# A hybrid network of eight stages on one core: heads and row sums from one product, sums and shifts made inside other stages, router joined with experts, one scan input in sixteen made by VectorE

## The reference

```python
x = L0_attn_a_x
x = x + l0_attn_a(layernorm(x))   # 16-head attention + state-space scan + gated MLP
x = x + l0_ffn(layernorm(x))      # two layers: window attention, gated MLP
x = x + attn_b(layernorm(x))      # 16-head causal attention
x = x + l0_ffn(layernorm(x))
x = x + l1_attn_a(layernorm(x))   # 16-head causal attention, rotary, biases on q, k, v and output
x = x + l1_ffn(layernorm(x))      # 8 experts, the best two of each token count
x = x + l1_attn_b(layernorm(x))   # random features
x = x + l1_ffn(layernorm(x))
# a head of attention (8 features):  softmax(q k^T / sqrt(8)) v
# the scan:   h = exp(dt*A)*h + dt*b*x ;  y = sum(h*c)   over 256 steps, 128 x 128 states
# a window layer first shifts features 64..127 by one token:
#             t2 = pad(t2)[:, :-1] ; h = concat(t1, t2)
# experts:    tgt2 = sum_e gate_e * (relu(x W1_e + b1_e) W2_e + b2_e) ; layernorm(tgt + tgt2)*gamma + beta
```

## Time and profile before

| | us |
|---|---|
| median of three runs (6312.53 to 6316.73) | 6315.28 |
| the profiled execution, its own time | 6308.24 |
| its span, first to last instruction | 6306.2 |
| three attention stages | 302.1, 306.4, 320.8 |
| scan_stage | 1218.0 |
| one window_attention_stage (of four) | 427.3 |
| one experts_stage (of two) | 465.7 |

### The profile page before, as it was taken

How to read it: one execution, slowest core, us unless ns; L and a number is a source line. 1 busy time by engine, 2 the same in 40 slices (tenths; PEclk the granted TensorE clock), 3 DMA queues, 4 the chain that set the end, 5 groups by cost and what they waited for, 6 DMA issues and landing times. The chain is left out here.

```text
span 6306.2 us, 119595 instructions
## 1 busy us (share of the span) xinstructions
PE 5418.4 (86%) x42357; PEld 2908.8 (46%) x42357; DVE 3589.7 (57%) x4103; ACT 3331.1 (53%) x4993; POOL 2512.4 (40%) x1721
## 2 busy tenths in 40 slices
PE   6876888888887998998898998999897999776998
PEld 2432555555544553564344554554343444343443
DVE  4557999999954554554344554554454343554344
ACT  4555888888854553554444554454343333443343
POOL 1223999999933651652122661662221000000000
PEclk8996999999998999999899999999899999998999
DMA  1002111101011110110000110110000210001121
GB/s 41 1 0 77 31 32 30 33 30 33 29 47 29 40 40 14 41 41 13 1 0 18 45 40 12 42 40 20 28 0 8 54 40 13 0 0 27 32 36 27
DMA packets 136966, 171.03 MB, mean 27 GB/s; under 512 B 32352, under 2 KB 85728, under 8 KB 135520
## 3 DMA queue, kind: packets, MB, share of 16 engines
q1 hardware_dynamic: 136800, 168.85, 10.2%
HBM read 80.11 MB, written 12.85 MB: 15 GB/s over the span
## 5 line engine op out<-in xcount | busy, mean ns | idle before, releaser
L2318 POOL TENSOR_TENSOR arena<-arena,wbig 128x1024 f32<-128x1024 f32 x512 | 1191.8, 2515 | 103.5 <-DMA wbig<-scratch_b 100.3
L2305 DVE TENSOR_TENSOR_SCAN arena<-banks,arena 128x1024 f32<-128x1024 f32 x512 | 1141.5, 2279 | 63.7 <-ACT banks L2249 45.5
L944 ACT ACTIVATE arena<-banks,wbig 128x512 f32<-128x512 f32 x512 | 352.0, 688 | 584.3 <-PE banks L907 572.7
L601 DVE TENSOR_REDUCE arena<-banks 128x4 f32<-128x1024 f32 (+1 forms) x384 | 401.9, 1047 | 432.8 <-PE banks L435 305.1
L957 DVE TENSOR_TENSOR arena<-arena 128x512 f32<-128x512 f32 x512 | 353.3, 692 | 490.2 <-ACT arena L944 434.7
L768 POOL TENSOR_TENSOR X<-X,Z 128x1536 f32<-128x1536 f32 x2 | 9.5, 4758 | 1482.6 <-ACTq L761 1482.6
L1462 POOL TENSOR_TENSOR arena<-arena 128x512 f32<-128x512 f32 x256 | 355.5, 1389 | 594.5 <-DMA arena<-arena 594.5
L2249 ACT ACTIVATE banks<-banks 128x1020 f32<-128x1020 f32 x512 | 518.2, 1012 | 104.3 <-PE banks L2170 96.8
L2254 ACT COPY arena<-banks 128x1024 f32<-128x1024 f32 x512 | 520.8, 1017 | 51.4 <-POOL arena L2318 30.8
L547 ACT ACTIVATE Y<-banks 128x2048 f32<-128x2048 f32 x192 | 305.8, 1593 | 408.4 <-PE banks L471 311.4
L907 PE MATMUL banks<-Z,wbig 128*128 x1024 | 462.2, 597 | 34.3 <-ACTq L56 34.3
(11 more groups left out here) (289 smaller groups left out, 10428.3 us busy)
## 6 DMA issues: line engine op xcount, KB each, us to landing
arena<-arena SPq DMA_DIRECT2D x1024, 64.0 KB, 2.0
arena<-scratch_g SPq DMA_DIRECT2D x32, 1024.0 KB, 13.8
wbig<-scratch_d SPq DMA_DIRECT2D x512, 16.0 KB, 1.7
wbig<-scratch_b SPq DMA_DIRECT2D x64, 128.0 KB, 2.2
wbig<-scratch_c SPq DMA_DIRECT2D x64, 128.0 KB, 2.1
arena<-Z SPq DMA_DIRECT2D x64, 128.0 KB, 2.1
wbig<-in_l_ffn SPq DMA_DIRECT2D x1, 4197.0 KB, 12.9
X<-in_x SPq DMA_DIRECT2D x2, 2048.0 KB, 14.7
```

The lines of the kernel that those rows point to most:

```text
L601: dve.tensor_reduce(to, mbank[:, :, :, 0:keys], AX_X, ALU.max).then_inc(dve_m.sem, 1)
L944: act.activation(hid[e % 2][:, f, :], hbank[f], ACT.Relu, bias=b1[:, e, f:f + 1])\
L2305: dve.tensor_tensor_scan(own, line(decay_bank[n % 2]), own, 0.0, ALU.mult, ALU.add)\
L2318: pool.tensor_tensor(four(h[par][:, m * 1024:m * 1024 + 1024]), four(us[n % 2]), Bs[par].unsqueeze(1).to_broadcast([128, 4, SEQ]), ALU.mult)\
```

## The change

1. `attention_stage`: the value operand `vm` has, beside the 8 value columns of a head, 8 columns of ones, so one product gives values and row sums in alternating groups of 8 rows. The 8 products with `slot_ones` per round are gone. The result is now 128 x 512 per batch (two halves, heads of even and odd pairs) and goes to two buffers. DVE copies it out of PSUM (`heads_raw`), ACT makes Ln and Exp over all 512 columns (now after the second exponential and its shifts), SP moves the reciprocals 8 partitions up with one transfer per batch (`moved_to`), DVE multiplies twice 256 columns. `qb` and `km` have two buffers.
2. The output projections take two products per tile, one for each half. The bias of v is folded into the output bias once (`carried_bias_stage`).
3. `add_stage` is gone: the sums are made in the last product stage (gated_mlp_stage, step "both") or the last norm_stage (`add_to`).
4. `shift_stage` is gone: POOL writes the shifted copy in the stage that makes the source.
5. Router and experts are one block, `mixture_stage`; the gates are spread in four transfers of two experts.
6. In the scan DVE makes the input product of unit 12 of 16, POOL the other 15.

```diff
 def values(i, par, s):     # attention_stage, PE
                 for u in range(2):
                     j = 2 * jj + u
                     for g in range(4):
-                        pe.matmul(obank[rows(g), first:SEQ], vm[par][:, c, j, rows(g)], prob[s % 2][:, g, u, first:SEQ],
-                                  start=(s == 0 and u == 0), stop=True, skip_group_check=True)
-                    for g in range(4):
-                        last = pe.matmul(obank[rows(g), SEQ + first:2 * SEQ], k.c["slot_ones"][:, rows(j)],
-                                         prob[s % 2][:, g, u, first:SEQ], start=False, stop=True,
+                        last = pe.matmul(obank[rows(g), jj * SEQ + first:(jj + 1) * SEQ], vm[par][:, c, j, rows(g)],
+                                         prob[s % 2][:, g, u, first:SEQ], start=(s == 0 and u == 0), stop=True,
                                          skip_group_check=True)
...
+            def heads_raw(b):      # DVE
+                dve.wait_ge(pe_s.sem, pe_s.at(b + 1, "late"))
+                dve.wait_ge(dve_o.sem, dve_o.at(b, "out"))
+                dve.tensor_copy(raw, obank).then_inc(dve_o.sem, 1)
+
             def heads_out(b):
-                dve.wait_ge(act_s.sem, act_s.at(b + 1, "recip"))
-                to = out[:, bass.ds(b * SEQ, SEQ)]
-                dve.tensor_tensor(to, obank[:, 0:SEQ], recip, ALU.mult).then_inc(dve_o.sem, 1)
-                if bv is not None:
-                    dve.wait_ge(dve_o.sem, dve_o.at(b, "out"))
-                    dve.tensor_scalar(to, to, bv, None, ALU.add).then_inc(dve_o.sem, 1)
-
+                dve.wait_ge(moved.sem, moved.at(b * 16 + 16))
+                for jj in range(2):
+                    part = slice(jj * SEQ, (jj + 1) * SEQ)
+                    last = dve.tensor_tensor(outs[jj][:, bass.ds(b * SEQ, SEQ)], raw[:, part], moved_to[:, part],
+                                             ALU.mult)
+                last.then_inc(dve_o.sem, 1)
+
+            def trip(b, more):
+                if more:
+                    reduce(b + 1, 0)
+                heads_raw(b - 1)
+                if more:
+                    for n in range(1, 8):
+                        reduce(b + 1, n)
+                heads_out(b - 1)
...
+        @block.sync
+        def _(sp):
+            for b in range(BATCH):
+                sp.wait_ge(act_s.sem, act_s.at(b + 1, "recip"))
+                sp.wait_ge(dve_o.sem, dve_o.at(b, "out"))
+                sp.dma_start(moved_to[0:128 - HEAD_DIM, :], recip[HEAD_DIM:128, :]).then_inc(moved.sem, 16)
...
+            def shift_sum(b):      # window_attention_stage, POOL, after low(b + 2, 3)
+                pool.wait_ge(dve_y.sem, dve_y.at(b, "sum"))
+                for to, own in shifted_parts(shifted, y, b * SEQ, SEQ):
+                    pool.tensor_copy(to, own).then_inc(pool_h.sem, 1)
...
+                    for e in ex:   # mixture_stage, ACT
+                        if first and u == 0 and e == 2:
+                            act.wait_ge(chain.sem, chain.at(16))
+                            act.activation(ex_, diff, ACT.Exp).then_inc(weighed.sem, 1)
                         for f in quads:
...
+DVE_FED = (12,)
...
             with dve.Fori(0, trips) as t:      # scan_stage
                 for n in range(16):
-                    own = h[n // units][:, n % units * 1024:n % units * 1024 + 1024]
-                    dve.wait_ge(fed.sem, fed.at(t, n))
+                    if n in DVE_FED:
+                        dve.wait_ge(b_in[n // units].sem, b_in[n // units].at(t))
+                        dve.wait_ge(read.sem, read.at(t, n // units - 2))
+                        feed(dve, dve_fed, t, n)
+                    wait_fed(dve, t, n)
                     dve.wait_ge(decayed.sem, decayed.at(t, n))
```

More of the change, by code:

```diff
@@ L559, in trip @@
                 exponential(i, 0)
+                exponential(i, 1)
+                shifts(i, 1)
                 if back:
+                    logarithm(i - 1)
                     reciprocal(i - 1)
@@ new lines, in _ @@
+            for par in range(2):
+                trip(par, par, first=True)
+            with pool.Fori(1, BATCH // 2) as ii:
+                for par in range(2):
+                    trip(ii * 2 + par, par)
+        @block.sync
[4 more added lines that the diff above has]
+                sp.dma_start(moved_to[0:128 - HEAD_DIM, :], recip[HEAD_DIM:128, :]).then_inc(moved.sem, 16)
@@ new lines, in carried_bias_stage, with _ @@
+def carried_bias_stage(k, name, parts, bias):
+    made, done = Count(k, "carried", 1), Count(k, "carried_added", 1)
+    with k.nc.Block() as block:
+        @block.tensor
+        def _(pe):
+            for n, (w, b) in enumerate(parts):
+                last = pe.matmul(k.psum[:, 0, 0:1], w, b, start=(n == 0), stop=(n == len(parts) - 1))
+            last.then_inc(made.sem, 1)
+        @block.vector
+        def _(dve):
+            dve.wait_ge(made.sem, made.at(1))
+            dve.tensor_tensor(bias, k.psum[:, 0, 0:1], bias, ALU.add).then_inc(done.sem, 1)
+            dve.wait_ge(done.sem, done.at(1))
@@ L881, in experts_stage @@
     dve_s = Steps(k, "gated", dve_steps, trips)
-    spread = [Landed(k, f"gates_spread{u}", 2, trips) for u in two]
+    landed = [[Landed(k, f"gates_spread{u}_{q}", 1, trips) for q in quads] for u in two]
     hid = [k.arena.take(4 * TILE).rearrange("p (f t) -> p f t", f=4) for _ in two]
@@ L897, in _ @@
             pe_s.prime(pe)
+            for u in range(2):
+                for c in range(4):
+                    last = pe.matmul(lbank[u][32 * c:32 * c + 32, :], w["wr"],
+                                     z[:, (4 * u + c) * TILE:(4 * u + c + 1) * TILE], start=True, stop=True,
+                                     tile_position=(0, 32 * c))
+                last.then_inc(looked.sem, 1)
             def hidden(i, u, e):
@@ new lines, in _ @@
+            dve.memset(spread, 0.0).then_inc(chain.sem, 1)
+            for u in range(2):
+                dve.wait_ge(looked.sem, looked.at(u + 1))
+                dve.transpose(turned[:, u * TILE:(u + 1) * TILE], lbank[u]).then_inc(chain.sem, 1)
+            dve.wait_ge(chain.sem, chain.at(3))
+            dve.tensor_tensor(lg, slots(turned), br, ALU.add).then_inc(chain.sem, 1)
+            dve.wait_ge(chain.sem, chain.at(4))
+            pick(4, lg, top[0], first)
+            dve.scalar_tensor_tensor(out=rest, in0=first, scalar=NEG, in1=lg, op0=ALU.mult, op1=ALU.add)\
+                .then_inc(chain.sem, 1)
@@ L950, in _ @@
+            dve.tensor_tensor(first, first, wide(g1), ALU.mult).then_inc(chain.sem, 1)
+            dve.wait_ge(chain.sem, chain.at(19))
+            dve.tensor_tensor(second, second, wide(g2), ALU.mult).then_inc(chain.sem, 1)
+            dve.wait_ge(chain.sem, chain.at(21))
+            dve.tensor_tensor(slots(spread), first, second, ALU.add).then_inc(chain.sem, 1)
+            dve.wait_ge(chain.sem, chain.at(22))
+            dve.transpose(G, spread).then_inc(chain.sem, 1)
             with dve.Fori(0, trips) as i:
@@ L996, in more_groups @@
         "br": np.tile(i[A + "br"].reshape(1, -1), (128, 1)), "gamma": column(i[A + "gamma"]), "beta": column(i[A + "beta"])}
+    for which in ("attn_b", "l1_attn_a"):
+        own = groups[which]
+        own["wo0"], own["wo1"] = by_pair_rows(own.pop("wo"))
+    own["bv0"], own["bv1"] = by_pair_rows(own.pop("bv"))
     groups["l0_ffn"] = l0_ffn_group(i)
@@ L2115, in ssm_delta_stage @@
     k.arena.used = at
+DVE_FED = (12,)
+POOL_FED = tuple(n for n in range(16) if n not in DVE_FED)
 def scan_stage(k, name, xh, w, cst, selected, out, big):
```

382 lines of the change are left out of this document (194 added, 188 removed).

## The result

The changed kernel took 6198.42 us, the median of four runs (6197.10 to 6200.95), the kernel before on the same chip 6313.90 (6310.63 to 6316.73): a ratio of 0.982, 95% interval 0.980 to 0.984. It is faster by 115 us where 151 were forecast: inside the stated range of 6115 to 6220, outside the forecast of 6135 to 6180. The attention gained what was forecast, the router a little more. The scan lost 64 us where 8 were forecast.

The account below looks back on a forecast made before the run. Limits differ by stage: POOL's input products in the scan, a PE-DVE loop with PE's queue later in attention. Terms -115 + 21 + 2 - 31 - 26 - 10 + 8 = -151 us gave 6164; range 6115 to 6220.

Parts of the forecast that it names:

- DVE's new work: First attention: copy out of PSUM, 0.69 us, and two multiplications, 0.85 for the pair, per batch; free in masked attentions.
- The ends: Each attention ends later by copy, lookups, transfer and multiplications, with more memsets at the start: 4 us, three times 12.
- The rival in which DVE bounds the attention: Attentions: reductions, copy and multiplications on DVE leave half the gain, 57 us less, time 6221; chance 0.12.
- what the shifted copies leave: Stages that write shifted copies: POOL's last copies stand behind the stage, 8 us over eight places.
- The transfer's 9 us: Router with experts: the first gate transfer, with a quarter of the bytes, lands some 9 us sooner.
- the chain is 4 us later: Router: the Exp stands behind eight Relus that end some 13 us into the block, so the chain is 4 us later.
- a scan stage above 1250 us: Scan: one of the measurements named beforehand as showing the prediction wrong, as was a stage below 1205 us.
- I take the middle, 1.9: Scan: DVE's product priced between 1.2 to 1.3 us alone and 2.4 blocked; 61 us less 53 idle, 8 more.
- the row that described this place: Scan: the same sum on DVE and POOL, where the second to start stands still; gives DVE's product 2.4 us.
- scan pays in full: Scan: DVE's idle time can't be taken and each product is blocked; up to 77 us, time 6180 to 6233; chance 0.28.
- the attention's upper bound: Three attentions: 140 us less if every group of products with ones counts fully.
- the scan's lower bound: Scan: 11 us less, if products cost 1.3 us each and all of DVE's idle time is used.

Follow-up runs that it names:

- the run with doubled values: Changed kernel with each group of four value products in the three attentions issued twice, values and sums doubled alike: 6289.7 us, ratio 0.996.
- the two runs: Changed kernel with value products issued twice, 6289.7 us; and changed kernel with one `km` and one `qb` again, 6233.8 us.
- the run with halves: Changed kernel with the gates spread by two transfers of four experts, DVE's first multiplication waiting for both: 6213.1 us, ratio 0.984.
- three forms with short products on DVE: Changed kernel with unit 12's product ahead of scan 11, 6139.8 us; that plus the copy's own place, 6138.3; that early order for units 4 and 12, 6139.0.

## Why the prediction was right, and where not

**Attention, -115 forecast, -116.6 measured: right, in its parts too.** The products with ones are worth 84 us by the run with doubled values (forecast 3.0 and 1.6 us a batch, 99 us), the second `km` 34 (forecast 38). DVE's new work, put at 1.5 us a batch in the first attention (24 us), seems to cost less: if the two runs add up, 39.2 + 16.5 - 50.2 is 5 us, where 50.2 is the gain of 46.4 and the 3.8 by which the stage ends later behind its last exponential. The ends are 10 us longer in the three, forecast 12. The rival in which DVE bounds the attention did not come about.

**Output stages and bias, +23 forecast, +22.3 measured.** Right.

**Adds, -31 forecast, -31.2 measured; shifts, -26 and -23.9.** The stages gave what their rows said. The term that was small is what the shifted copies leave, 8 us forecast and 11 measured: the two gated MLPs that write one are 2.4 and 2.7 us longer, where a tail of 1.0 was forecast, and the norm stage ahead of the second `l0_ffn`'s first window attention 3.4, at a clock of 0.90 for 1.00. Not in the sum at all were the norm stages behind the window attentions, 10.8 us less, by the clock; the earlier trace rows showed the shift stage at a clock of 0.68, and I read nothing from it.

**Router, -10 forecast, -17.0 measured.** The transfer's 9 us are right (8.8 by the run with halves). The failed term is "the chain is 4 us later": the Exp ran at 11.2 us into the block, 1.9 later than before, since ACT's Relus come every 0.86 us and the eighth ended at 11.3, not "some 13 us". The first multiplication came 6.9 us sooner in the first block (27.8 for 34.7 us) and 10.0 in the second (26.1 for 36.1), and the blocks are 7.6 and 9.4 us shorter.

**Scan, +8 forecast, +64.3 measured: here the prediction failed, in the size of two terms, and one of its own signs of being wrong, a scan stage above 1250 us, came true.** The step was: "I take the middle, 1.9, times 32 is 61 us, less the 53 us of idle time if DVE uses all of it". The price was 2.24 us each time, 72 us: between ends far apart the row that described this place gave 2.4, and the middle was not called for. And the idle time was not used as a sum: the stage's idle time stayed at 70 us. It is not that it can't be used. Early products of 1.20 us found it, 32 or 64 of them, for under 10 us. A product of 2.24 us behind scan 11 finds some 1.1 us of it in trips at the full clock, and about as much is paid; then DVE has next to no room left, and 13 trips of 31, those with the lower clock, are 2.1 us longer still. The rival "scan pays in full" had the right price and size (77 us at most), but not this second half.

That the product would be blocked each time is what the Trainium skill says (SBUF — State Buffer, Who interferes with whom): a DVE instruction with two SBUF inputs and a GpSimd one that reads SBUF exclude each other for a whole instruction, and one with at most one SBUF input does not. The traces agree on both: 2.24 us with two, 1.21 with one, in the same place beside the same product of POOL. Had I gone by the page, the scan term would have been +24 with all idle time used.

**The sum.** With the scan as forecast the time would have been some 56 us less, 6142, inside the forecast. As measured it lies where the rival "scan pays in full" put it, 6180 to 6233; the range held it because it was drawn to take in most of that rival. Its lower end, 6115, is a slip: the attention's upper bound alone gives 6164 - 25 = 6139, with the scan's lower bound 6120.

**What stays open.** Which trips the clock falls in, and where in a trip, was not settled: a pause of 2.1 to 2.5 us stands in all of them, and the clock falls in kernels without it. So the 27 us of the 13 trips are argued. My theory that the late release of `us` is a cause was wrong: with the copy in a place of its own the stage was 7 to 15 us longer than without. Why longer, and not equal, I read as the clock (0.88 in the stage, for 0.93), no more.

**The best form** is the changed kernel with no blocked product in the scan. With all products on POOL it took 6135 and 6138 us, some 60 under the changed one; three forms with short products on DVE (6138 to 6140) are not to be told from it.

## What to carry to other kernels

Work taken from the bounding engine is worth something only if its price where it lands is its unblocked price: look at what the neighbour runs at the moment at which it starts, not at its price alone. An engine's idle time is no store to draw on as a sum; a short delay is taken up by the next gap, and a long one is paid for what the gaps don't hold, and leaves no room for the next wait. And a stage in which TensorE does nothing costs more than its length, which the clock column of the stage behind it shows.

## What the runs showed of the hardware

Two products with two SBUF inputs each, one on DVE and one on POOL, don't run beside each other: the later one waits for the whole of the earlier (2.06 and 2.24 us for 1.20 on DVE, 2.7 for 2.4 and 3.35 for 2.4 on POOL, by how much was left of the other). Multiplications of 256 columns went from 0.42 to 1.44 us in the same way. TensorE's granted clock fell in the loop of the scan, about once a trip of 37 us, also where its longest pause in a trip was 1.0 us; the stage's mean was the same 0.93 with pauses of 2.1 to 2.5 us in every trip and without. What a fall cost was not the same; that it depends on the room that the engine behind has left is my reading.
